# A recommender's last batch norm: one dependent VectorE step skipped, the norm put before another chunk's weighted sum, and two of four last chunks summed on TensorE

## What is computed

```
E    = concat(cat_t2[f, cat], cont_t2 * cont)            # 2048 x 39 x 64
fm   = sum(first order terms) + 0.5 * sum(s*s - sum(E*E))   # s = sum over fields
h    = relu(batchnorm(E.reshape(2048, 2496) @ W1 + b1, g1, be1))   # 1024 wide
h    = relu(batchnorm(h @ W2 + b2, g2, be2))                       # 512 wide
y    = sigmoid(bias + fm + h @ W3 + b3)                             # 2048
out  = [1 - y, y]
batchnorm(x, g, b) = g * (x - mean) * rsqrt(var + 1e-5) + b        # mean, var over the batch
```

## Time and profile before

| what | us |
|---|---|
| median of 3 runs | 634.28 (634.26 to 634.67) |
| the profiled execution | 634.16 |
| its span, first to last instruction | 632.4 |
| TensorE busy | 558.0 (88%) |
| ScalarE busy | 212.2 (34%) |
| VectorE busy | 149.5 (24%) |
| GpSimd busy | 393.9 (62%) |
| mean granted TensorE clock | 0.984 |

### The profile page before, as it was taken

One profiled execution on the slowest core, in us unless ns is written; L12 is line 12 of the kernel. 1 busy time (PEld: TensorE's weight loads), 2 busy tenths in 40 slices (PEclk: granted clock), 3 DMA queues, 4 the chain that ended last, 5 costly groups with the idle time before them and its releaser, 6 DMA issues.

```text
span 632.4 us, 8548 instructions
## 1 busy us (share of the span) xinstructions
PE 558.0 (88%) x2531; PEld 447.7 (71%) x2531; DVE 149.5 (24%) x473; ACT 212.2 (34%) x682; POOL 393.9 (62%) x423
## 2 busy tenths in 40 slices
PE   6999897779878977798779878998899999999998
PEld 1488786668666866686658666776678876888887
DVE  2101130013001201130004000311122204755265
ACT  1223132223222322232223222322222415998565
POOL 5777777777777777777777777777777771000000
PEclk9789999999999999999999999989998999999998
DMA  8963343334432343334423432363334321000000
GB/s 257 353 128 27 28 27 27 27 26 28 27 28 26 27 28 27 27 27 27 27 26 27 28 26 27 27 160 27 27 27 28 28 27 8 1 2 0 1 0 2
DMA packets 18251, 26.79 MB, mean 42 GB/s; under 512 B 7827, under 2 KB 8059, under 8 KB 18236
## 3 DMA queue, kind: packets, MB, share of 16 engines
q0 software_dynamic: 13312, 13.87, 28.7%
q1 hardware_dynamic: 4608, 12.66, 5.7%
q10 hardware_dynamic: 316, 0.07, 0.1%
HBM read 26.56 MB, written 0.02 MB: 42 GB/s over the span
## 4 chain that ended last, share of the span: by engine, by line
PE 42%; DMA 33%; issue 13%; POOL 7%; ACT 2%; DVE 1%; POOLq 1%; ACTq 1%; DVEq 0%; SPq 0%
DMA emb<-in_table,idx_now 32%; PE bank L726 16%; PE bank L799 14%; POOL emb L251 7%; PE bank L767 4%; PE bank L700 2%; ACT junk L289 2%; PE bank L717 2%; PE bank L757 1%; PE bank L835 1%; DMA h<-in_w 1%; DVE idx_now L468 1%; PE bank L848 1%; PE bank L758 0%; ACTq L289 0%
## 5 line engine op out<-in xcount | busy, mean ns | idle before, releaser
L251 POOL DMA_INDIRECT emb<-in_table,idx_now x416 | 393.1, 945 | 129.7 <-issue 111.2
L726 PE MATMUL bank<-x_sb,w_sb 128*128 128x256 f32 x1664 | 381.2, 384 | 2.4 <-ACT x_sb L282 2.4
L726 PEld LDWEIGHTS bank<-x_sb,w_sb 128*128 128x128 f32 x1664 | 312.7, 192 | 43.2 <-ACT x_sb L282 3.6
L289 ACT ACTIVATE junk<-emb 128x128 bf16<-128x128 f32 x208 | 64.2, 309 | 254.8 <-DMA emb<-in_table,idx_now 242.5
L487 DVE TENSOR_TENSOR bank<-emb,bank 128x260 f32<-128x260 f32 x91 | 39.3, 432 | 319.6 <-DMA emb<-in_table,idx_now 319.6
L717 PE MATMUL bank<-ident,emb 128*128 128x128 f32 x208 | 44.0, 294 | 61.5 <-DMA emb<-in_table,idx_now 59.9
L717 PEld LDWEIGHTS bank<-ident,emb 128*128 128x128 f32 x208 | 22.9, 141 | 91.9 <-DMA emb<-in_table,idx_now 82.7
L282 ACT ACTIVATE x_sb<-bank 128x256 f32<-128x256 f32 x104 | 38.3, 369 | 64.0 <-PE bank L717 64.0
L799 PE MATMUL bank<-hhi,w2hi 128*128 128x512 f32 x128 | 50.5, 395 | 0.4 <-issue 0.4
L799 PE MATMUL bank<-hhi,w2lo 128*128 128x512 f32 x128 | 50.7, 396 | 0.0
L799 PE MATMUL bank<-hlo,w2hi 128*128 128x512 f32 x128 | 39.0, 396 | 0.0
(11 more groups left out here) (79 smaller groups left out, 176.3 us busy)
## 6 DMA issues: line engine op xcount, KB each, us to landing
emb<-in_table,idx_now POOLq DMA_INDIRECT x416, 3.3
w_sb<-in_w SPq DMA_DIRECT2D x13, 512.0 KB, 18.2
h<-in_w SPq DMA_DIRECT2D x6, 512.0 KB, 7.7
w2raw<-in_w SPq DMA_DIRECT2D x8, 256.0 KB, 5.6
h<-in_w SPq DMA_DIRECT2D x1, 256.0 KB, 12.3
idx_all<-in_cat SPq DMA_DIRECT2D x1, 182.0 KB, 3.0
cont_sb<-in_cont_t SPq DMA_DIRECT2D x8, 13.0 KB
diag<-in_cont_diag ACTq DMA_DIRECT2D x1, 45.5 KB, 2.1
```

The lines of the kernel that those rows point to most:

```text
L251: nc.gpsimd.indirect_dma_start(out=emb[:, j, at:at + ROW], out_offset=None, in_=table, in_offset=bass.IndirectOffsetOnAxis(ap=idx_now[:, j ...
L289: nc.scalar.activation(junk[:, :], emb[:, j, k * PAIR + 1:k * PAIR + 1 + P], ACT.Square, accum_out=esq[:, ds(b * BT + j, 1), k]).then_inc( ...
L726: return nc.tensor.matmul(acc[c], w1_sb[:, k, c * P:(c + 1) * P], x_sb[:, k, :], start=False, stop=stop, skip_group_check=True)
```

## The change

`norm` gets a sixth row of scratch, MEAN. Where there is a bias (layer two), mean + bias is computed by an instruction of its own, before the wait for the square root. Where a part has one column, MEAN_SCALE is computed as reciprocal * g * mean, which no longer reads SCALE, so there is no wait between the two; where a part has more columns the chain stays as it was. The weighted sum of part 2, chunk 3 moves from before the last norm to behind `out_shift`. `ADDED_BY_PE` becomes 2, so that chunks 0 and 1 of part 3 are summed directly. The wide products before part 3 become 3, and those behind its chunk 0 go.

```diff
-WARM_PRODUCTS = 11
-BETWEEN = 2
-ADDED_BY_PE = 1
+WARM_PRODUCTS = 3
+ADDED_BY_PE = 2
...
-    bn2 = place("bn2", [P, 5, C2], f32)
+    bn2 = place("bn2", [P, 6, C2], f32)
...
-    STD, RSTD, SCALE, MEAN_SCALE, SHIFT = range(5)
+    STD, RSTD, SCALE, MEAN_SCALE, SHIFT, MEAN = range(6)
...
             def norm(bn, mv, bias, g, be, lo, hi, std_ready, part_no, norm_ready):
+                mean, one = mv[:, lo:hi, 0], hi - lo == 1
+                if bias is not None:
+                    chained(nc.vector.tensor_tensor(bn[:, MEAN, lo:hi], mean, bias[:, lo:hi], ALU.add))
+                    mean = bn[:, MEAN, lo:hi]
                 dve.wait_ge(std_ready, part_no + 1)
                 chained(nc.vector.reciprocal(bn[:, RSTD, lo:hi], bn[:, STD, lo:hi]))
-                chained(nc.vector.tensor_tensor(bn[:, SCALE, lo:hi], g[:, lo:hi], bn[:, RSTD, lo:hi], ALU.mult))
-                if bias is None:
-                    chained(nc.vector.tensor_tensor(bn[:, MEAN_SCALE, lo:hi], mv[:, lo:hi, 0],
+                scaled = nc.vector.tensor_tensor(bn[:, SCALE, lo:hi], g[:, lo:hi], bn[:, RSTD, lo:hi], ALU.mult)
+                if one:
+                    steps[0] += 1
+                    scaled.then_inc(norm_step, 1)
+                    chained(nc.vector.scalar_tensor_tensor(
+                        out=bn[:, MEAN_SCALE, lo:hi], in0=bn[:, RSTD, lo:hi], scalar=g[:, lo:hi],
+                        in1=mean, op0=ALU.mult, op1=ALU.mult))
+                else:
+                    chained(scaled)
+                    chained(nc.vector.tensor_tensor(bn[:, MEAN_SCALE, lo:hi], mean,
                                                     bn[:, SCALE, lo:hi], ALU.mult))
-                else:
-                    chained(nc.vector.scalar_tensor_tensor(
-                        out=bn[:, MEAN_SCALE, lo:hi], in0=mv[:, lo:hi, 0], scalar=bias[:, lo:hi],
-                        in1=bn[:, SCALE, lo:hi], op0=ALU.add, op1=ALU.mult))
...
                 mean2(m)
-                if m == C2 - 1:
-                    weighted(m - 1, N2 - 1)
                 norm(bn2, mv2, b2, g2, be2, m, m + 1, std2_ready, m, norm2_ready)
...
                                            op0=ALU.mult, op1=ALU.add).then_inc(shift_ready, 1)
+            weighted(m - 1, N2 - 1)
             for n in range(ADDED_BY_PE, N2):
                 weighted(m, n)
...
-            keep_warm(WARM_PRODUCTS)
+            for _ in range(WARM_PRODUCTS):
+                nc.tensor.matmul(bank[C2 + 1][:, :], w2hi[:, 0, 0:P], hhi[:, 0, :], start=True, stop=True)
             m = C2 - 1
             for n in range(ADDED_BY_PE):
                 pe.wait_ge(out2_ready, m * N2 + n + 1)
                 z_parts(m, n, w3[:, m:m + 1], True)
-                keep_warm(BETWEEN)
```

More of the change, by code:

```diff
@@ L845, in _ @@
                 z_parts(0, n, ones[:, :])
-            def keep_warm(times):
-                for _ in range(times):
-                    nc.tensor.matmul(bank[C2 + 1][:, :], w2hi[:, 0, 0:P], hhi[:, 0, :], start=True, stop=True)
-            keep_warm(WARM_PRODUCTS)
+            for _ in range(WARM_PRODUCTS):
+                nc.tensor.matmul(bank[C2 + 1][:, :], w2hi[:, 0, 0:P], hhi[:, 0, :], start=True, stop=True)
             m = C2 - 1
```

## The result

The change takes 634.95 us, the median of 22 runs (634.06 to 635.70), against 634.23 (22 runs, 633.30 to 635.03) for the kernel before. The ratio is 1.0012, with a 95% interval of 1.0007 to 1.0018: within 0.2%, and a little slower.

What follows compares the result with a forecast made beforehand. The prediction took TensorE's closing column products, at their own rate and granted clock, as the bound. From 634.16 profiled, 0.75 for the earlier clock fall net of gains plus 0.12 to the median gave 635.0; range 633.2 to 635.9.

Steps and rivals of the forecast that it cites:

- The moved weighted sum: VectorE, last norm: the reciprocal no longer waits behind the sum of part 2, chunk 3; gain 0.28 us.
- The skipped dependence: VectorE, norm: MEAN_SCALE no longer waits for SCALE, starting 0.08 instead of 0.19 us after it; gain 0.11, bounds 0 and 0.19.
- The first ReLU of part 3: ScalarE, after the last norm: starts 0.39 us earlier, at 624.20, by both VectorE gains; near 624.1 with layer one's.
- The first layer: VectorE, norms of parts 0 and 1: 0.05 us gained in each, 0.1 through to the end; bounds 0 and 0.25.
- TensorE's last 16 records: TensorE's end: column products of the last two chunks start at 627.25, less 0.1; over 3.3 us at half clock.
- The clock: TensorE's tail: fewer wide products let the clock halve earlier, so the products end 0.75 us later, at 630.9; chance 0.50.
- The formula's lower bound: TensorE's end: the products end no earlier than 630.65 if the last 16 records all take 0.21 us each.
- At full clock: TensorE's end: with no clock fall the products would end at 629.07, 1.08 us earlier than before.
- the case with the last 8 records slow: TensorE's end: the clock holds until the last 8 records; time 634.0 us, within the full-clock rival's 0.22 chance.
- the early fall: TensorE, before 625.65: the clock falls before part 3's direct sums, nearly all 32 records slow; 636.0 us; chance 0.20.
- my bound for slower: Whole kernel: times over 635.55 us count as slower, 0.2% beyond the kernel before; chance 0.20.
- The rival in which the clock stays full: TensorE's tail: full clock to the end or until 628.1 or later; 633.2 us, 634.0 with 8 slow records; chance 0.22.

Runs made afterwards that it cites:

- e3: The kernel before with 3 wide products instead of 11 and none behind the direct sum; 636.49 us, ratio 1.0028.
- e6: The change with the old norm and the weighted sum in its old place, so only TensorE's part; 636.24 us, ratio 1.0029.
- e11_before_width64: The kernel before with column products 64 columns wide, 63 of them zeros; 743.25 us on the slow chip, ratio 0.9998.
- e1: The change with 5 wide products instead of 3 ahead of part 3 and 1 behind the direct sums; 635.37 us, ratio 1.0007.
- e2: The change with no wide products ahead of part 3 instead of 3; 635.65 us, ratio 1.0018.
- e8: The change with column products 64 columns wide, 63 of them zeros, same number, order and waits; 633.64 us, ratio 0.9991.
- e5: The kernel before with only VectorE's part of the change: new norm and moved weighted sum; 634.27 us, ratio 0.9999.
- e11_added1_wide9_between2: The change with one direct chunk, 9 wide products ahead of part 3 and 2 behind the direct sum; 633.89 us, ratio 0.9992.
- e9: The change with column products 16 columns wide, 15 of them zeros; 743.91 us on the slow chip, ratio 1.0003.
- the last four: The 16- and 64-column kernels timed on the slow chip, e9, e11_before_width64 and e12 among them; 740.91 to 744.50 us.
- e12: e8 with three direct chunks instead of two and no wide products; 740.91 us on the slow chip, ratio 0.9963.

## Why the prediction was right

The forecast was a change within 0.2%, slightly slower, at 635.0; measured were 634.95 and 1.0012.

- *The moved weighted sum* was to bring the reciprocal to 623.47, less 0.1 for layer one. It stands at 623.37. The added instruction is covered by the square root, as said.
- *The skipped dependence* was put at 0.11 by the pair of the earlier trace rows: SCALE to MEAN_SCALE went from 0.19 to 0.08. The Trainium skill's sentence on chaining ("VectorE: DVE Perf Modes", The DRAIN you can't avoid), by which it brings nothing, does not hold here; the same section also says that an operation which is not held starts earlier, and that fits this pair.
- *The first ReLU of part 3*: predicted near 624.1, measured 624.08.
- *The first layer*, 0.1: the first column product is 0.11 earlier, 621.88 against 621.99. Since that point moves by up to 1.0 us between profiles, this alone would prove nothing. The waits do: in the four profiles with the old `norm` (before, e3, e6 and e11_before_width64) TensorE waits 0.41 us before its first product of layer two and 0.38 for the first low half, in the ten with the new one 0.34 or 0.35 and 0.31 or 0.32. Together 0.12 to 0.14.
- *TensorE's last 16 records*: predicted from about 627.15, measured 627.14.
- *The clock*: predicted to fall at 625.7 to 626.8, middle 626.25; in the profile it fell at 626.4. 13 of the 32 records were issued by then. The formula's lower bound, 630.65, applies; the products ended at 630.72. My middle, 630.9, was 0.2 too late.
- *At full clock* the change was to gain 1.08 against the profiled execution, 0.41 of it the slow records of the kernel before. That leaves 0.67. With 64 columns in both kernels the clock stays out of it: the tails of 7.23 and 7.81 differ by 0.58, and with the 0.1 from layer one that makes 0.7. The step holds, on one profile of each.

So the change gains 0.7 and pays for it: in the profiles the thin filling costs it 8.84 - 7.23 = 1.6 us, against 8.16 - 7.81 = 0.35 in the kernel before.

The mechanism was right, and the exact hit was partly luck. I moved two delays of one trace (3.7 and 2.3 us behind wide products) to the new place, took the middle, and the two bracketed the fall. Neither came true by itself: in the change the fall came 4.5 us behind the end of layer two's products, not 3.7, and about 1.9 behind the three wide ones, not 2.3. In e1 it came 1.8 us behind the last of five, and in e2 2.4 us behind the end of layer two. In the three profiles with one column and three wide products (the change, e3, e6) it lies 4.3 to 4.6 us behind the first column product. Single runs of the change reach from 634.06 to 635.70, from about the case with the last 8 records slow (634.0) into that of the early fall; 2 of 22 lie over my bound for slower, 635.55. The rival in which the clock stays full was argued from the rows and stood beside the Trainium skill's rule on idle gaps between bursts ("TensorE: Matmul & The Clock Gate", Why this matters for your kernels). It did not happen with one column, though TensorE was never idle for long: 0.34 us, at 624.61, is the longest gap in the changed kernel's tail. It came true in e8, where the products were wide, with the same gap of 0.34 and one more of 0.20.

## What to carry to other kernels

Where TensorE ends a kernel with many products of one column, look at the granted clock of that stretch, not at its busy time; half a clock doubled the distance between the records of these products from 0.11 to 0.21 us. Before you trim products that only fill time, price what they hold up, and before you add more of them, see whether the products that count can be made wider at little cost, as 64 columns were here, and time it: 16 columns did not hold the clock in their one profile, and neither did 64 without the wide products in front. A gain on one engine arrives only if the next engine isn't busy with its own filling when it comes (e5 against e11_added1_wide9_between2).

## What I had not expected

- 63 columns of zeros were enough in e8; columns of other values were not tried. They lengthened the distance of the records from 0.112 to 0.115 us: (2.00 - 0.28) / 15.
- Five wide products and one more bought 0.3 us of clock, eleven some 3 us (4.9 and 7.9 after the first column product, against 4.5; one profile each, so the 0.3 may be chance).
- The end of layer two moved by 1.0 us between profiles (first column product at 621.75 to 622.76), though the kernels differ by only 0.1 us up to there. In e1, e3 and e6 the gap between the last gather and the statistics behind it was 0.3 longer too. The cause stays open.
- On one chip every version took 741 to 745 us: GpSimd's gather instructions were as long as elsewhere (945 ns), but in e9's profile it sat idle before them for 235 us instead of 130. In all four the whole difference lies before layer two. Why is open; it was the reason that the last four could not be timed to 0.1%.
- Whether e12 beats e8 and e11_added1_wide9_between2 in time is open for the same reason; its ratio of 0.9963 on that chip (2.7 us) is more than its tail, 7.00 against 8.16, can give, and I don't count it.
